# Graph layer with a normalised residual: adjacency kept in DRAM as fp32r and loaded tile by tile, self projection kept in SBUF

## The chip, the cores and the metric

The kernel runs on one core of one Trainium2 chip. The metric is the device time of one execution in microseconds (us); the median of three runs of the kernel before is 1660.79 us (1660.56 to 1660.93).

## The reference

`x` is (8, 2048, 512), the adjacency `a` is 2048 x 2048 of 0 and 1 (the same for all batches), `W` is 512 x 1024. Everything is fp32.

```python
Wi, Wj = (W[:, :Din], W[:, Din:])
mi = jnp.einsum('bkd,od->bko', x, Wi)
mj = jnp.einsum('bkd,od->bko', x, Wj)
deg = a.sum(axis=1)
out = deg[None, :, None] * (mi + b) + jnp.einsum('ij,bjo->bio', a, mj)
x = _layernorm(x + out, axis=-1)
```

## The kernel before

A batch has 16 row tiles of 128 rows. For each of the 8 batches two stages follow one another on TensorE.

**Projection**, 16 tiles of two halves (h = 0 gives `mj`, h = 1 gives `mi`). To keep fp32 accuracy with fp32r products, `x` and `W` are split in high and low parts. A half has 4 cross products (L295) and 8 main products (L305, L307), all 128x128 by 128x512. ScalarE makes `x_hi` and `x_lo` (L380, L382), copies the cross products out of PSUM (L395) and rounds `mj` to `mj_hi` (L399); POOL makes `x_df` and `mj_lo` (L247, L252); VectorE splits x and combines `mj` and `mi` (L489, L492, L502, L510). `mi` is a single tile: SP stores it to a DRAM buffer (L193), and `combine_mi` waits for the store of the tile before (L509).

**Aggregation**, 16 tiles. Tile i multiplies 16 weight tiles of the transposed adjacency (`adjT[s]`, two buffers of 128 x 2048 fp32r, 1 MB) with `mj_hi` and `mj_lo`: 32 matmuls (L329) in one of two PSUM banks. The adjacency lies in SBUF as int8 (`adjT8`), and ScalarE widens one tile at a time (`widen`, L411) when the tile two before has been multiplied. SP loads `mi` back into `mi_in` (L177) and x into `r` (L180); POOL adds the bias to `mi_in` (L258); VectorE makes the residual (L538), then in `normalise` adds the PSUM result (L544), takes the statistics, waits for the root from ScalarE (`root`, L415) and scales; SP stores the tile (L225). TensorE's tile m waits for the sum of tile m-2 (L321).

In **batch 0** the adjacency also comes in: 64 chunks of 128 x 512 int32 (256 KB) through four buffers `adj_in` (L164). ScalarE casts each to int8 (`cast_chunk`, L406), VectorE adds it up for the degrees (`count_chunk`, L521, L524). Two chunks go with each projection tile, and the other 32 with the aggregation tiles by this list:

```python
AGG_CHUNKS = [0, 3, 3, 3, 3, 2, 2, 4, 4, 4, 4, 0, 0, 0, 0, 0]
```

Every engine's order is the order in the program text, for SP too: one list of waits and transfers. `load_chunk(c)` waits until ScalarE and VectorE have used chunk c-4 (L162, L163). In an aggregation tile, ScalarE casts that tile's chunks, widens, and then does `root`; VectorE counts the tile's chunks, then does the next residual and `normalise`.

Of the kernel before, what the change touches and what calls it, by code (L numbers as in the profile page):

```python
# [5 lines left out]
def bass_adj_resnorm(nc, x, xt, adjt, wt, b, out):  # L6
# [32 lines left out]
    with ctx:  # L39
# [9 lines left out]
        mi_dram = nc.dram_tensor("mi_dram", [TILES, P, DO], fp32, kind="Internal").ap()  # L49

        adjT8 = sb("adjT8", [P, NT, N], i8)
# [13 lines left out]
        mi = sb("mi", [P, DO], fp32)  # L65
        mi_in = [sb(f"mi_in{s}", [P, DO], fp32) for s in range(2)]
# [20 lines left out]
        w_stage = [r[0], r[1], r[2], r[3], mi_in[0], mi_in[1], deg_part, mi]  # L87
# [20 lines left out]
        mi_stored = sem("mi_stored")  # L108
        mi_loaded = [sem(f"mi_loaded{s}") for s in range(2)]
# [6 lines left out]
        adjT_ready = sem("adjT_ready")  # L116
# [14 lines left out]
        AGG_CHUNKS = [0, 3, 3, 3, 3, 2, 2, 4, 4, 4, 4, 0, 0, 0, 0, 0]  # L131
# [26 lines left out]
        @block.sync  # L158
        def _(sp):
            def load_chunk(c):  # L160
                if c >= AB:
                    sp.wait_ge(adj_cast, c - AB + 1)  # L162
                    sp.wait_ge(deg_part_ready, c - AB + 1)  # L163
                sp.dma_start(adj_in[c % AB][:, :], adjt[c // NT, c % NT]).then_inc(adj_loaded[c % AB], 16)  # L164

            sp.dma_start(x_raw[0][:, :], xt[0]).then_inc(x_loaded[0], 16)
            for c in range(DK, 2 * DK):
                sp.dma_start(w_stage[c][:, :], wt[c]).then_inc(w_loaded[c], 16)
            sp.dma_start(x_raw[1][:, :], xt[1]).then_inc(x_loaded[1], 16)
            for c in range(DK):  # L170
                sp.dma_start(w_stage[c][:, :], wt[c]).then_inc(w_loaded[c], 16)
# [4 lines left out]
            def load_mi(m, u):  # L176
                sp.dma_start(mi_in[u % 2][:, :], mi_dram[m]).then_inc(mi_loaded[u % 2], 16)  # L177

            def load_r(m, u):
                sp.dma_start(r[u][:, :], x_tiles[m]).then_inc(r_loaded[u], 16)  # L180

            def batch(bt):
                zero = known(bt) and bt == 0
                base = NT * bt

                def proj(g):
                    for u in range(GT):
                        n = base + GT * g + u
                        if zero:
                            for c in range(PROJ_CHUNKS * (GT * g + u), PROJ_CHUNKS * (GT * g + u + 1)):  # L190
                                load_chunk(c + AB)
# [3 lines left out]
                over_groups(sp, zero, False, proj)  # L195

                sp.wait_ge(mi_stored, 16 * (base + 2))
                for u in range(2):
                    load_mi(base + u, u)
                for u in range(GT - 1):  # L200
                    if not zero:
                        sp.wait_ge(out_stored[u], 16 * NG * bt)
                    load_r(base + u, u)

                def agg(g):
                    for u in range(GT):
                        i = GT * g + u
                        m = base + i
                        begin = known(g) and g == 0
                        ending = known(g) and g == NG - 1  # L210
                        if begin and u == 0:
                            sp.wait_ge(mi_stored, 16 * (base + NT))
# [24 lines left out]
            for u in range(GT):  # L237
                sp.wait_ge(out_stored[u], 16 * NG * NB)

        @block.gpsimd  # L240
        def _(pool):
# [14 lines left out]
            def add_bias(m, u, turn):  # L256
                pool.wait_ge(mi_loaded[u % 2], turn)
                pool.tensor_tensor(mi_in[u % 2][:, :], mi_in[u % 2][:, :], bias[:, :], ALU.add).then_inc(mib_ready, 1)  # L258
# [3 lines left out]
            def batch(bt):  # L262
# [13 lines left out]
                with pool.Fori(0, NP) as k:  # L276
                    for u in range(2):
                        add_bias(NT * bt + 2 * k + u, u, 16 * (NP * bt + k + 1))
# [4 lines left out]
        def _(pe):  # L283
# [34 lines left out]
            def aggregate(bt, i, s, first, wait_free):  # L318
# [15 lines left out]
            def batch(bt):  # L334
# [13 lines left out]
                if zero:  # L348
                    for i in range(NT):
# [6 lines left out]
                        aggregate(0, i, i % 2, i == 0, i >= 2)  # L356
                else:
                    for i in range(2):
                        aggregate(bt, i, i, i == 0, True)
                    with pe.Fori(1, NP) as k:  # L360
                        for i in range(2):
                            aggregate(bt, 2 * k + i, i, False, True)
# [8 lines left out]
        def _(act):  # L371
# [52 lines left out]
            def batch(bt):  # L424
# [3 lines left out]
                def proj(g):  # L428
                    last_group = known(g) and g == NG - 1
                    for u in range(GT):  # L430
# [13 lines left out]
                        if last_group and u in (0, 2):  # L444
                            widen(u // 2, u // 2, NT if zero else None)

                over_groups(act, zero, True, proj)
                if zero:
                    for i in range(NT):
                        for c in agg_chunks(i):  # L450
                            cast_chunk(c)
                        if i < NT - 2:
                            act.wait_ge(agg_done, i + 1)
                            widen(i + 2, i % 2, NT * ((i + 2) // TPB + 1))
                        root(i)
                else:
                    with act.Fori(0, NP - 1) as k:
                        for i in range(2):
                            m = NT * bt + 2 * k + i
                            act.wait_ge(agg_done, m + 1)  # L460
                            widen(2 * k + i + 2, i, None)
                            root(m)
                    for i in range(2):
                        root(NT * bt + NT - 2 + i)
# [4 lines left out]
        def _(dve):  # L469
            def split_w(c, order):  # L470
# [5 lines left out]
                nc.vector.tensor_scalar(top[:, :].bitcast(u32), w_stage[c][:, :].bitcast(u32),  # L476
                                        HI_BITS, None, ALU.bitwise_and).then_inc(w_top_ready, 1)
                dve.wait_ge(w_top_ready, order + 1)
                nc.vector.tensor_tensor(W_lo[:, c, :], w_stage[c][:, :], top[:, :], ALU.subtract).then_inc(w_lo_ready, 1)  # L479
# [25 lines left out]
            def combine_mi(n):  # L505
                dve.wait_ge(main_done, 2 * n + 2)
                dve.wait_ge(cross_ready, 2 * n + 2)
                if not (known(n) and n == 0):
                    dve.wait_ge(mi_stored, 16 * n)  # L509
                nc.vector.scalar_tensor_tensor(mi[:, :], main_ps[1][:, :], 1.0 + 1.0 / S, cross[1][:, :],  # L510
# [22 lines left out]
            def residual(m, i, u, turn):  # L533
# [4 lines left out]
                nc.vector.scalar_tensor_tensor(r[u][:, :], mi_in[u % 2][:, :], deg[:, bass.ds(i, 1)], r[u][:, :],  # L538
# [35 lines left out]
            def batch(bt):  # L574
# [3 lines left out]
                def proj(g):  # L578
                    for u in range(GT):
# [7 lines left out]
                        combine_mi(n)  # L587
# [67 lines left out]
```

## Time and profile before

| What | us |
|---|---|
| median of the runs | 1660.79 |
| the profiled execution | 1659.85 |
| its span, first to last instruction | 1658.0 |
| TensorE busy | 1639.1 |
| VectorE busy | 851.4 |
| ScalarE busy | 665.0 |
| POOL busy | 504.9 |

The span is the time from the first to the last instruction of the profiled execution; its own time has 1.85 us around that. The granted TensorE clock is 0.996 of full speed in the mean. The DMA engines moved 187.26 MB, at 113 GB/s in the mean. A busy share says how much an engine worked, and not that the end waits for it: the chain that ended last and the waits tell that.

### The profile page before, as it was taken

The page shows a single profiled execution, that of the slowest core. Times are in us where ns is not written, and L with a number is a line of the kernel's source. Part 1 is how long each engine was busy: PE and PEld are TensorE (multiplying, and loading weights), DVE is VectorE, ACT ScalarE, POOL GpSimd, SP SyncE. Part 2 cuts the span into 40 slices and gives each one's busy share as a digit, 9 for nine tenths or more (in the row PEclk, how much of TensorE's full clock was granted, in tenths as well). Part 3 has the DMA queues.
Part 4 walks back from the last instruction along what each step waited for, and adds up shares of the span by engine and source line. Part 5 has one row for each costly group of instructions (what it writes and reads, how often), then busy time and mean ns, then how long its engine had stood idle before and what let it go on. Part 6 is the DMA issues. An engine that isn't in the chain of part 4 may idle for free.

```text
span 1658.0 us, 24935 instructions
## 1 busy us (share of the span) xinstructions
PE 1639.1 (99%) x7248; PEld 1354.8 (82%) x7248; DVE 851.4 (51%) x1884; ACT 665.0 (40%) x970; POOL 504.9 (30%) x390
## 2 busy tenths in 40 slices
PE   7999999999999999999999999999999999999998
PEld 5888888888888888888888888888888888888886
DVE  7768754455444544444544554444454445444544
ACT  5665435423344323442345332453225533255221
POOL 2542124311343113431134311443114421144210
PEclk8999999999999999999999999999999999999999
DMA  5656522333224332333322432224322343232432
GB/s 172 190 185 221 187 81 89 126 115 101 81 97 126 108 108 76 101 127 108 98 85 94 128 106 95 90 93 133 109 87 89 101 129 105 82 102 82 127 114 70
DMA packets 102698, 187.26 MB, mean 113 GB/s; under 512 B 11408, under 2 KB 11408, under 8 KB 102672
## 3 DMA queue, kind: packets, MB, share of 16 engines
q1 hardware_dynamic: 84528, 153.92, 29.0%
q10 hardware_dynamic: 18144, 33.04, 6.5%
q8 instruction: 11, 0.18, 0.0%
q14 instruction: 15, 0.12, 0.0%
HBM read 119.80 MB, written 67.11 MB: 113 GB/s over the span
## 4 chain that ended last, share of the span: by engine, by line
PE 96%; DVE 1%; DMA 1%; issue 1%; ACT 0%; SPq 0%; POOL 0%; DVEq 0%; ACTq 0%
PE agg_ps L329 56%; PE main_ps L305 13%; PE main_ps L307 13%; PE cross_ps L295 13%; DMA mi_dram<-mi 1%; DVE W_lo L479 0%; DVE deg_part L524 0%; PE deg_ps L314 0%; DMA mi_in<-in_wt 0%; ACT x_lo L382 0%; DVE mj L476 0%; DVE cross L476 0%; DVE mi L510 0%; DVE deg_part L521 0%; DVE x_raw L492 0%
## 5 line engine op out<-in xcount | busy, mean ns | idle before, releaser
L329 PE MATMUL agg_ps<-mj_lo,adjT 128*128 128x512 f32 x2048 | 797.9, 390 | 0.0
L329 PE MATMUL agg_ps<-mj_hi,adjT 128*128 128x512 f32 x2048 | 797.8, 390 | 0.0
L411 ACT ACTIVATE adjT<-adjT 128x2048 fp32r (+1 forms) x128 | 245.3, 1917 | 552.1 <-PE agg_ps L329 552.1
L329 PEld LDWEIGHTS agg_ps<-mj_hi,adjT 128*128 128x128 f32 x2048 | 384.4, 188 | 79.9
L329 PEld LDWEIGHTS agg_ps<-mj_lo,adjT 128*128 128x128 f32 x2048 | 384.8, 188 | 79.3
L305 PE MATMUL main_ps<-W_hi,x_hi 128*128 128x512 f32 x1024 | 400.0, 391 | 1.4 <-DVE mi L510 1.4
L307 PE MATMUL main_ps<-W_lo,x_lo 128*128 128x512 f32 x1024 | 399.7, 390 | 0.0
L258 POOL TENSOR_TENSOR mi_in<-mi_in,bias 128x512 f32<-128x512 f32 x128 | 166.0, 1300 | 651.3 <-DMA mi_in<-mi_dram 651.3
L295 PE MATMUL cross_ps<-W_df,x_df 128*128 128x512 f32 x1024 | 275.8, 392 | 9.6 <-POOL x_df L247 8.2
L252 POOL TENSOR_TENSOR mj_lo<-mj,mj_hi 128x512 f32 (+1 forms) x128 | 172.4, 1347 | 277.6 <-ACT mj_hi L399 277.6
L544 DVE TENSOR_TENSOR r<-agg_ps,r 128x512 f32<-128x512 f32 x128 | 88.4, 691 | 316.7 <-PE agg_ps L329 316.6
L395 ACT ACTIVATE cross<-cross_ps 128x512 f32<-128x512 f32 x256 | 150.6, 588 | 214.5 <-PE cross_ps L295 210.3
L295 PEld LDWEIGHTS cross_ps<-W_df,x_df 128*128 128x128 f32 x1024 | 192.0, 188 | 52.4 <-issue 8.3
L247 POOL TENSOR_TENSOR x_df<-x_top,x_lo 128x512 fp32r<-128x512 f32 x128 | 166.3, 1299 | 203.9 <-ACT x_lo L382 203.6
L305 PEld LDWEIGHTS main_ps<-W_hi,x_hi 128*128 128x128 f32 x1024 | 192.7, 188 | 42.5 <-DVE mi L510 2.3
L307 PEld LDWEIGHTS main_ps<-W_lo,x_lo 128*128 128x128 f32 x1024 | 193.0, 188 | 40.0
L502 DVE SCALAR_TENSOR_TENSOR mj<-main_ps,cross 128x512 f32<-128x512 f32 x128 | 88.3, 690 | 206.2 <-PE main_ps L307 199.2
L510 DVE SCALAR_TENSOR_TENSOR mi<-main_ps,cross 128x512 f32<-128x512 f32 x128 | 88.5, 691 | 129.4 <-PE main_ps L307 109.1
L538 DVE SCALAR_TENSOR_TENSOR r<-mi_in,deg,r 128x512 f32<-128x512 f32 x128 | 96.5, 756 | 53.8 <-DMA r<-in_x 43.1
L380 ACT ACTIVATE x_hi<-x_top 128x512 fp32r<-128x512 f32 x128 | 80.8, 631 | 65.5 <-PE main_ps L307 63.8
L546 DVE BATCH_NORM_STATS2 stats<-r 128x6 f32<-128x512 f32 x128 | 88.9, 695 | 11.6
L492 DVE TENSOR_TENSOR x_raw<-x_raw,x_top 128x512 f32<-128x512 f32 x128 | 88.7, 693 | 4.4
(43 smaller groups left out, 586.5 us busy)
## 6 DMA issues: line engine op xcount, KB each, us to landing
mi_dram<-mi SPq DMA_DIRECT2D x128, 256.0 KB, 2.0
mi_in<-mi_dram SPq DMA_DIRECT2D x128, 256.0 KB, 2.7
r<-in_x SPq DMA_DIRECT2D x128, 256.0 KB, 2.7
out<-r SPq DMA_DIRECT2D x128, 256.0 KB, 2.0
x_raw<-in_xt ACTq DMA_DIRECT2D x126, 256.0 KB, 2.7
adj_in<-in_adjt SPq DMA_DIRECT2D x64, 256.0 KB, 3.1
r<-in_wt SPq DMA_DIRECT2D x4, 256.0 KB, 5.3
x_raw<-in_xt SPq DMA_DIRECT2D x2, 256.0 KB, 3.8
```

Source lines behind the costliest of these rows:

```text
L247: pool.tensor_tensor(x_df[s][:, :], x_top[:, :], x_lo[s][:, :].bitcast(fp32), ALU.subtract).then_inc(x_df_ready, 1)
L252: pool.tensor_tensor(mj_lo[:, bass.ds(t, 1), :].rearrange("p t d -> p (t d)"), mj[:, :], mj_hi[:, bass.ds(t, 1), :].rearrange("p t d -> p ...
L258: pool.tensor_tensor(mi_in[u % 2][:, :], mi_in[u % 2][:, :], bias[:, :], ALU.add).then_inc(mib_ready, 1)
L295: last = nc.tensor.matmul(cross_ps[h][:, :], x_df[s][:, k * P:(k + 1) * P], W_df[:, half * DK + k, :], start=(k == 0), stop=(k == DK - 1))
L305: nc.tensor.matmul(main_ps[h][:, :], x_hi[s][:, k * P:(k + 1) * P], W_hi[:, half * DK + k, :], start=(k == 0), stop=False)
L307: last = nc.tensor.matmul(main_ps[h][:, :], x_lo[s][:, k * P:(k + 1) * P], W_lo[:, half * DK + k, :], start=False, stop=(k == DK - 1))
L329: last = nc.tensor.matmul(agg_ps[s][:, :], adjT[s][:, j, :], part[:, j, :], start=(j == 0 and part is mj_hi), stop=(j == NT - 1 and part i ...
L395: nc.scalar.activation(cross[h][:, :], cross_ps[h][:, :], ACT.Copy).then_inc(cross_ready, 1)
L411: nc.scalar.activation(adjT[s][:, :, :], adjT8[:, :, bass.ds(i * P, P)], ACT.Copy).then_inc(adjT_ready, 1)
L492: nc.vector.tensor_tensor(x_raw[s][:, :], x_raw[s][:, :], x_top[:, :], ALU.subtract).then_inc(x_rest_ready, 1)
L538: nc.vector.scalar_tensor_tensor(r[u][:, :], mi_in[u % 2][:, :], deg[:, bass.ds(i, 1)], r[u][:, :], ALU.mult, ALU.add).then_inc(res_ready, 1)
L546: nc.vector.bn_stats(stats[:, :], r[u][:, :]).then_inc(ln_step, 1)
```

## The change

- `mi_dram`, `mi_in` and `adjT8` go. `mi` becomes 16 tiles in SBUF (32 KB a partition); `combine_mi` writes tile t of it without a wait for a store, POOL adds the bias in place, the residual reads it there. Three of the staging buffers for W are now slices of `mi`.
- In batch 0 `cast_chunk` makes fp32r instead of int8, into one of two buffers `adj_wide`; ScalarE then waits for its own cast and itself issues the store of the chunk to `adj_dram`, in four pieces a partition of 128 values (512 B) each. The cast of chunk c waits for the store of chunk c-2.
- `widen` goes. SP loads `adjT[s]` from `adj_dram` in two halves of 512 KB (rows of 4 KB): the first when half of the tile two before has been multiplied (a new semaphore, `half_done`), the second when all of it has. TensorE waits for the halves one by one. The last two tiles of a batch load tiles 0 and 1 of the next. In batch 0 the first two tiles are loaded behind projection tile 10, and a load waits until the chunks that it reads are stored.
- The first three `r` tiles of a batch are loaded ahead of SP's wait in the aggregation rather than behind its projection loop, which is gone.
- The chunks of batch 0 go with the aggregation tiles by another list.

```diff
-        AGG_CHUNKS = [0, 3, 3, 3, 3, 2, 2, 4, 4, 4, 4, 0, 0, 0, 0, 0]
+        AGG_CHUNKS = [0, 3, 3, 3, 3, 4, 4, 4, 4, 4, 0, 0, 0, 0, 0, 0]
...
+            def load_adjT(i, s, q, zero):
+                if zero:
+                    for w in range(2):
+                        sp.wait_ge(adj_stored[w], 16 * (NT * (i // TPB) + NP * (q + 1)) // 2)
+                sp.dma_start(adjT[s][:, NP * q:NP * (q + 1), :].bitcast(fp32),
+                             adj_dram[i, :, NP * q:NP * (q + 1), :]).then_inc(adjT_loaded[s][q], 16)
...
-                        sp.wait_ge(mi_ready, n + 1)
-                        sp.dma_start(mi_dram[n], mi[:, :]).then_inc(mi_stored, 16)
...
+                if zero:
+                    for t in range(NT):
+                        for c in range(PROJ_CHUNKS * t, PROJ_CHUNKS * (t + 1)):
+                            load_chunk(c + AB)
+                        if t == 10:
+                            for i in range(2):
+                                for q in range(2):
+                                    load_adjT(i, i, q, True)
...
-                        if not (ending and u >= GT - 2):
-                            sp.wait_ge(res_ready, m + 1)
-                            load_mi(m + 2, u)
+                        wraps = ending and u >= GT - 2
+                        if not (last_batch and wraps):
+                            sp.wait_ge(half_done, m + 1)
+                            load_adjT(u - 2 if wraps and u >= 2 else i + 2, u % 2, 0, zero and not wraps)
+                            sp.wait_ge(agg_done, m + 1)
+                            load_adjT(u - 2 if wraps and u >= 2 else i + 2, u % 2, 1, zero and not wraps)
...
-                pe.wait_ge(adjT_ready, m + 1)
+                pe.wait_ge(adjT_loaded[s][0], turn)
                 if first:
                     pe.wait_ge(mj_lo_ready, NT * bt + NT - 1)
                 for j in range(NT):
+                    if j == NP:
+                        pe.wait_ge(adjT_loaded[s][1], turn)
...
+                    if j == NP - 1:
+                        last.then_inc(half_done, 1)
                 last.then_inc(agg_done, 1)
...
             def cast_chunk(c):
-                s = c % AB
+                s, w = c % AB, c % 2
+                q, j = c // NT, c % NT
                 act.wait_ge(adj_loaded[s], 16 * (c // AB + 1))
-                q, j = c // NT, c % NT
-                nc.scalar.activation(adjT8[:, j, q * DO:(q + 1) * DO], adj_in[s][:, :], ACT.Copy).then_inc(adj_cast, 1)
-
-            def widen(i, s, chunks):
-                if chunks is not None:
-                    act.wait_ge(adj_cast, chunks)
-                nc.scalar.activation(adjT[s][:, :, :], adjT8[:, :, bass.ds(i * P, P)], ACT.Copy).then_inc(adjT_ready, 1)
+                if c >= 2:
+                    act.wait_ge(adj_stored[w], 16 * (c // 2))
+                nc.scalar.activation(adj_wide[w][:, :], adj_in[s][:, :], ACT.Copy).then_inc(adj_cast, 1)
+                act.wait_ge(adj_cast, c + 1)
+                act.dma_start(adj_dram[TPB * q:TPB * (q + 1), :, j, :].rearrange("t p i -> p t i"),
+                              adj_wide[w][:, :].bitcast(fp32).rearrange("p (t i) -> p t i", t=TPB)
+                              ).then_inc(adj_stored[w], 16)
...
-            def combine_mi(n):
+            def combine_mi(n, t):
                 dve.wait_ge(main_done, 2 * n + 2)
                 dve.wait_ge(cross_ready, 2 * n + 2)
-                if not (known(n) and n == 0):
-                    dve.wait_ge(mi_stored, 16 * n)
```

## Rows read from the trace of the kernel before

**Rows 1.** The page: busy time and instructions, and the chain that ended last.
```profile
PE 1639.1 (99%) x7248; PEld 1354.8 (82%) x7248; DVE 851.4 (51%) x1884; ACT 665.0 (40%) x970; POOL 504.9 (30%) x390
...
PE 96%; DVE 1%; DMA 1%; issue 1%; ACT 0%; SPq 0%; POOL 0%; DVEq 0%; ACTq 0%
```
**Rows 2.** The chain in order of time: start us, us, what.
```profile
109.55 7.25 PE agg_ps L329 x32
...
228.46 0.91 PE cross_ps L295 x4
...
518.96 116.05 PE agg_ps L329 x512
...
722.37 116.05 PE agg_ps L329 x512
```
**Rows 3.** Timeline of TensorE, projection of batch 0: start us, us, instruction.
```profile
37.64 1.07 PE L295 MATMUL cross_ps<-W_df,x_df 128*128 128x512 f32 x4
...
41.66 1.07 PE L295 MATMUL cross_ps<-W_df,x_df 128*128 128x512 f32 x4
...
92.31 1.07 PE L295 MATMUL cross_ps<-W_df,x_df 128*128 128x512 f32 x4
...
95.03 1.07 PE L295 MATMUL cross_ps<-W_df,x_df 128*128 128x512 f32 x4
...
98.50 1.08 PE L295 MATMUL cross_ps<-W_df,x_df 128*128 128x512 f32 x4
```
**Rows 4.** The waits: total us, how many, longest.
```profile
ACT adjT L411 <- PE agg_ps L329: 552.1, 109, 8.1
...
DVE mi L510 <- DMA mi_dram<-mi: 18.1, 12, 3.3
```
**Rows 5.** The page's groups: busy us, mean ns | idle before, and its releaser.
```profile
L411 ACT ACTIVATE adjT<-adjT 128x2048 fp32r (+1 forms) x128 | 245.3, 1917 | 552.1 <-PE agg_ps L329 552.1
```
**Rows 6.** Windows: length, busy of PE, PEld, DVE, ACT, POOL; PEclk, DMA share, GB/s.
```profile
8.00:9.00 1.00, 0.00 (x0) 0.00 (x0) 0.97 (x3) 0.15 (x1) 0.00 (x0) 1.00 1.06 399
...
146.00:153.00 7.00, 7.00 (x33) 5.79 (x32) 6.16 (x15) 3.82 (x5) 1.29 (x1) 1.00 0.80 257
...
183.00:190.00 7.00, 7.00 (x33) 5.80 (x32) 6.05 (x15) 4.59 (x6) 1.59 (x1) 1.00 0.82 241
...
316.00:432.00 116.00, 116.00 (x514) 96.12 (x513) 57.11 (x153) 29.91 (x29) 21.06 (x17) 1.00 0.35 109
```
**Rows 7.** Timeline of VectorE in an aggregation tile of a middle batch.
```profile
424.46 0.69 DVE L544 TENSOR_TENSOR r<-agg_ps,r 128x512 f32<-128x512 f32 x1 [3.00 <-PE agg_ps L329]
...
427.88 0.55 DVE L563 TENSOR_SCALAR r<-r,mean_var,inv_std 128x512 f32<-128x512 f32 x1
```
**Rows 8.** DMA issues: count, KB each, median us from issue to landing.
```profile
r<-in_x SPq DMA_DIRECT2D x128, 256.0 KB, 2.7
out<-r SPq DMA_DIRECT2D x128, 256.0 KB, 2.0
...
adj_in<-in_adjt SPq DMA_DIRECT2D x64, 256.0 KB, 3.1
```
**Rows 9.** Timeline of ScalarE and its queue in a projection tile of batch 0.
```profile
52.80 0.63 ACT L380 ACTIVATE x_hi<-x_top 128x512 fp32r<-128x512 f32 x1 [0.24 <-PE main_ps L307]
53.34 0.62 ACT L382 ACTIVATE x_lo<-x_raw 128x512 fp32r<-128x512 f32 x1
...
53.98 0.33 ACTq L386 DMA_DIRECT2D x_raw<-in_xt  x1
...
56.37 0.60 ACT L395 ACTIVATE cross<-cross_ps 128x512 f32<-128x512 f32 x1 [1.37 <-PE cross_ps L295]
```
**Rows 10.** Timelines of ScalarE and VectorE, tiles with four chunks, batch 0.
```profile
171.56 0.20 ACT L415 ACTIVATE std<-var_eps 128x1 f32<-128x1 f32 x1
...
176.84 0.69 DVE L544 TENSOR_TENSOR r<-agg_ps,r 128x512 f32<-128x512 f32 x1
...
184.10 0.69 DVE L544 TENSOR_TENSOR r<-agg_ps,r 128x512 f32<-128x512 f32 x1
```

More of the change, by code:

```diff
@@ L64, in bass_adj_resnorm @@
         mj = sb("mj", [P, DO], fp32)
-        mi = sb("mi", [P, DO], fp32)
-        mi_in = [sb(f"mi_in{s}", [P, DO], fp32) for s in range(2)]
+        mi = sb("mi", [P, NT, DO], fp32)
+        adj_wide = [sb(f"adj_wide{s}", [P, DO], fp32r) for s in range(2)]
         r = [sb(f"r{s}", [P, D], fp32) for s in range(GT)]
@@ L85, in bass_adj_resnorm @@
         deg_ps = pb("deg_ps")
-        w_stage = [r[0], r[1], r[2], r[3], mi_in[0], mi_in[1], deg_part, mi]
+        w_stage = [r[s][:, :] for s in range(4)] + [mi[:, NT - 3, :], mi[:, NT - 2, :], deg_part[:, :], mi[:, NT - 1, :]]
         w_top = [mj, cross[1]]
@@ L107, in bass_adj_resnorm @@
         mi_ready = sem("mi_ready")
-        mi_stored = sem("mi_stored")
-        mi_loaded = [sem(f"mi_loaded{s}") for s in range(2)]
+        adj_stored = [sem(f"adj_stored{s}") for s in range(2)]
         r_loaded = [sem(f"r_loaded{s}") for s in range(GT)]
@@ L115, in bass_adj_resnorm @@
         deg_ready = sem("deg_ready")
-        adjT_ready = sem("adjT_ready")
+        adjT_loaded = [[sem(f"adjT_loaded{s}{q}") for q in range(2)] for s in range(2)]
+        half_done = sem("half_done")
         zeroed = sem("zeroed")
@@ L183, in batch @@
                 zero = known(bt) and bt == 0
+                last_batch = known(bt) and bt == NB - 1
                 base = NT * bt
[L186 to L191, printed above, removed]
-                        sp.wait_ge(mi_ready, n + 1)
-                        sp.dma_start(mi_dram[n], mi[:, :]).then_inc(mi_stored, 16)
[L195 to L199, printed above, removed]
+                if zero:
[6 more added lines that the diff above has]
+                                    load_adjT(i, i, q, True)
                 for u in range(GT - 1):
@@ L202, in batch @@
                         sp.wait_ge(out_stored[u], 16 * NG * bt)
+                    else:
+                        sp.wait_ge(w_ready, 2 * DK)
+                        sp.wait_ge(w_hi_ready, 2 * DK)
                     load_r(base + u, u)
@@ L254, in rest_of_mj, with add_bias @@
                                    ALU.subtract).then_inc(mj_lo_ready, 1)
-            def add_bias(m, u, turn):
-                pool.wait_ge(mi_loaded[u % 2], turn)
-                pool.tensor_tensor(mi_in[u % 2][:, :], mi_in[u % 2][:, :], bias[:, :], ALU.add).then_inc(mib_ready, 1)
+            def add_bias(m, i):
+                pool.wait_ge(mi_ready, m + 1)
+                own = mi[:, bass.ds(i, 1), :].rearrange("p t d -> p (t d)")
+                pool.tensor_tensor(own, own, bias[:, :], ALU.add).then_inc(mib_ready, 1)
             difference(0, 0)
@@ L277, in batch @@
                     for u in range(2):
-                        add_bias(NT * bt + 2 * k + u, u, 16 * (NP * bt + k + 1))
+                        add_bias(NT * bt + 2 * k + u, 2 * k + u)
             over_batches(pool, batch)
@@ L316, in degrees, with aggregate @@
                 last.then_inc(deg_in_psum, 1)
-            def aggregate(bt, i, s, first, wait_free):
+            def aggregate(bt, i, s, turn, first, wait_free):
                 m = NT * bt + i
@@ L355, in batch @@
                             degrees(3)
-                        aggregate(0, i, i % 2, i == 0, i >= 2)
+                        aggregate(0, i, i % 2, 16 * (i // 2 + 1), i == 0, i >= 2)
                 else:
                     for i in range(2):
-                        aggregate(bt, i, i, i == 0, True)
+                        aggregate(bt, i, i, 16 * (NP * bt + 1), i == 0, True)
                     with pe.Fori(1, NP) as k:
                         for i in range(2):
-                            aggregate(bt, 2 * k + i, i, False, True)
+                            aggregate(bt, 2 * k + i, i, 16 * (NP * bt + k + 1), False, True)
             pe.wait_ge(zeroed, 2)
@@ L451, in batch @@
                             cast_chunk(c)
-                        if i < NT - 2:
-                            act.wait_ge(agg_done, i + 1)
-                            widen(i + 2, i % 2, NT * ((i + 2) // TPB + 1))
                         root(i)
                 else:
[L457 to L464, printed above, removed]
+                    with act.Fori(0, NT) as i:
+                        root(NT * bt + i)
             over_batches(act, batch)
@@ L503, in combine_mj @@
                                                ALU.mult, ALU.subtract).then_inc(mj_ready, 1)
-            def combine_mi(n):
+            def combine_mi(n, t):
                 dve.wait_ge(main_done, 2 * n + 2)
                 dve.wait_ge(cross_ready, 2 * n + 2)
-                if not (known(n) and n == 0):
-                    dve.wait_ge(mi_stored, 16 * n)
-                nc.vector.scalar_tensor_tensor(mi[:, :], main_ps[1][:, :], 1.0 + 1.0 / S, cross[1][:, :],
+                nc.vector.scalar_tensor_tensor(mi[:, bass.ds(t, 1), :].rearrange("p t d -> p (t d)"), main_ps[1][:, :], 1.0 + 1.0 / S, cross[1][:, :],
                                                ALU.mult, ALU.subtract).then_inc(mi_ready, 1)
@@ L586, in proj @@
                             count_chunk(PROJ_CHUNKS * t)
-                        combine_mi(n)
+                        combine_mi(n, t)
                         if zero:
```

19 lines of the change are left out of this document (6 added, 13 removed).

## Prediction

> **What bounds the kernel now.** I read first the busy shares and the chain that ended last: TensorE is busy 1639.1 of 1658.0 us and holds 96% of the chain [rows 1]. So only what makes TensorE wait, or its work longer, counts. Next the chain in order of time, in a middle batch: from one aggregation's start to the next are 203.41 us, and its 512 matmuls take 116.05 [rows 2], that is 0.2267 us each and 7.25 us for a tile of 32. A projection tile has 24, 5.44 us. A batch of both is 16 x 12.69 = 203.1 us, so a middle batch has 0.3 us to give. All 7168 by 0.2267 are 1625 us; the 33 that are left lie at both ends of the kernel and in batch 0. The instructions, their shapes and the form of the weights in SBUF don't change, so I leave the 0.2267.
>
> Then TensorE's own timeline in batch 0. A half of a projection tile takes 2.72 us (95.03 - 92.31); twice it takes more, 41.66 - 37.64 = 4.02 and 98.50 - 95.03 = 3.47 [rows 3], together **2.05 us** lost. The waits say why: VectorE waited 18.1 us in 12 waits for the store of the single `mi` tile (L509) [rows 4], and the rest of that was covered. The longer waits beside it, ScalarE 552.1 us before the widening, are of an engine with time to spare.
>
> **The change, part by part.**
>
> *The widening (L411) goes.* 128 copies by 1.917 us are 245 us of ScalarE [rows 5]. TensorE never waits for them in a middle batch, where the period is the pure matmul time. Worth 0. The cover is TensorE itself.
>
> *The round trip of `mi` goes.* 128 stores and 128 loads of 256 KB leave SP's queue, and L509's wait goes: -2.05 us, all of it in batch 0. The store is late there because SP issues it behind adjacency chunks whose buffers it waits for. What is late next is the adjacency traffic below. The bias additions on POOL have the same number and now run back to back behind the projection; they stand beside VectorE work that in a middle batch waits for TensorE at each tile. 0 us.
>
> *The load of adjT, middle batches.* 256 issues of 512 KB replace the 256 of `mi`, so SP's issue time is no longer than before. Rate: 109 GB/s now in the aggregation [rows 6]; 16 loads of `mi` (4.2 MB in 116 us, 36 GB/s) go and 16.8 MB (145 GB/s) come: 218 GB/s, while 399 GB/s is shown for loads alone [rows 6]. Timing: SP does everything in order, so the first half of tile m+3 stands behind the store of tile m. That store is ready 3.97 us after the sum of m starts (427.88 + 0.55 - 424.46) [rows 7], so the load goes out at about +4.4 us and is needed at +14.5 (two tiles on). A 256 KB load lands in 2.7 us [rows 8]; half a tile adds another 0.7 us: 3.4 against 10 us. The second half has some 11 us. Tiles 0 and 1 of the next batch are fetched in the last two tiles of this one. 0 us.
>
> *Batch 0, projection.* ScalarE gets 32 stores. Each must wait until its own cast has ended (the starts of two ACTIVATEs are 0.54 apart and one takes 0.63, so 0.1 us) and issue; issuing took 0.33 us for the x load [rows 9]. Two chunks a tile add 0.9 us to an engine that idles 0.24 + 1.37 us a tile [rows 9]: covered, 0 us. Queued behind are the cross copies that TensorE's next half needs, so the bound from above is an issue four times as long (four times as many rows): 2.8 us a tile, 1.2 over, 19 us in 16 tiles. I take the 0.33, the one issue on this queue that a row shows. At the eleventh tile SP issues four half tiles ahead of the chunk loads: 2 MB, 5.6 us at the rate below, so a chunk lands after 3.1 + 5.6 = 8.7 us, and the four buffers give 4 x 2.72 = 10.9. 0 us, with 2.2 left.
>
> *Batch 0, aggregation.* Here I see the price. Count in pieces of 256 KB. A tile with four chunks has 4 chunk loads, 4 chunk stores, 4 for the next adjT tile, 1 for r and 1 for out; five tiles in a row have that. Before, with neither the stores nor the adjT loads beside them, the DMA share was already 0.80 and 0.82 at 257 and 241 GB/s [rows 6]. Four tiles have three chunks. Two prices are unknown. (a) The time of 256 KB with the DMA engines full: 0.66 us by the 399 GB/s of loads alone, 0.81 by the mixed row (257 / 0.80 = 321 GB/s). I take **0.70**, nearer the first, since reads outnumber stores. (b) What a store in rows of 512 B costs against one in rows of 2 KB; the trace has none. From below 1; from above 4, a short row as dear as a long one. The nearest row, the 2 KB-row store with 2.0 us to landing [rows 8], is mostly latency and not transfer, so I stay near the lower end: **1.25**. So with four chunks 10 + 5 = 15 pieces x 0.70 = 10.5 us against 7.26 of TensorE, 3.24 over, five times 16.2; with three chunks 9 + 3.75 = 12.75 x 0.70 = 8.93, 1.67 over, four times 6.7. Together the DMA engines fall **22.9 us** behind.
>
> The Trainium skill (DMA: Bandwidth & Descriptors, Why small descriptors are slow) gives about three bus cycles of overhead a packet at 32 bytes a cycle; an estimate by it is 76 / 67 = 1.13 for (b), the lag 20.2 and the end 1672. The same page (Specifications) puts HBM for one core at about 358 GB/s; the trace's 399 over one us disagrees, and with 358 the estimate would be 1679.
>
> How much lag is covered: the cast waits for the store two chunks back, `root(i)` is queued behind the casts on ScalarE, VectorE's normalise waits for root, the next sum is behind it, and TensorE's tile i+3 waits for that sum (L321). In batch 0 the root at 171.56 is followed by the sum at 176.84, done at 177.53; tile 10 needs it when tile 9 ends, at about 184.1 [rows 10]. **6.5 us** of cover. Nothing regains lag in between: at four chunks VectorE's own sums stand 7.25 us apart with no idle time noted before the two later ones [rows 10]. TensorE stalls 22.9 - 6.5 = 16.4 us, between tiles 6 and 12 of batch 0.
>
> **Sum.** -2.05 + 16.4 = +14.3 us. The profiled execution took 1659.85 us (1.85 around the span) and the median is 0.94 above it; 1659.85 + 14.3 = 1674.2, and on the median's footing **1675 us**, 0.9% slower.
>
> **Rivals.**
> *The cover holds (not slower).* For: at 0.66 us a piece and a factor of 1 the lag is (14 x 0.66 - 7.26) x 5 + (12 x 0.66 - 7.26) x 4 = 12.5 us, and part of it is adjT halves that can themselves be 7 us late without harm. It decides where the lag stays under about 8 us. Then -2.05 and up to 2 us of stall: 1659 to 1661 us. Against: it needs the best rate seen for 65 us on end. Chance 0.25. Within it lies the case that all is hidden, 1658.7; a gain over 0.2% would need 3.3 us, and rows give only the 2.05.
> *ScalarE's two store buffers set the pace, not the volume.* A chunk takes (cast 0.62 + 0.1 + issue 0.33 + landing) / 2. With the 2.0 of the 2 KB-row store it is 1.5 us, under the 1.8 that four chunks a tile allow; with 4 us (my estimate for the load there, from the 3.1 of a chunk load now [rows 8] and the traffic that comes) 2.5. Then 10.1 - 7.26 = 2.9 x 5 and 0.3 x 4, 15.5 - 6.5 = 9, less 2.05: 1668 us. Longest waits would be ScalarE's, for the stores, with the DMA share well below 1. Chance 0.20.
> *Short rows are dear.* Factor 2 and 0.81 a piece: (18 x 0.81 - 7.26) x 5 + (15 x 0.81 - 7.26) x 4 = 56 us, less 8.5: 1708 us. The DMA share would stay at 1 from tile 1 to 12. Chance 0.15.
>
> **How the numbers follow.** Forecast 0.40, rivals 0.25, 0.20, 0.15. About 0.2% (3.3 us) is what a measurement can tell. The first rival is nearly all "within", with 0.03 for a gain that I don't see; the others end slower, but 0.02 of the second may stay within: faster 0.03, same 0.24, slower 0.73. The range goes from the first rival's best case, 1658, to 1698, between the forecast and the dear store; what is left out is 0.12 above and a little below.
>
> **What would show it.** Right: middle batches still at 203.4 us a period; batch 0's aggregation at 130 to 140 us instead of 118.9 (228.46 - 109.55 [rows 2]), with TensorE's idle time before L321's tiles 6 to 12, DMA share near 1 there, ScalarE's casts waiting for chunk stores; projection of batch 0 some 2 us shorter. Wrong: a longer middle period (then a half tile is late and SP's order is to blame), stalls already in the projection (ScalarE's issue is dear, or the four early half tiles), or TensorE without gaps in batch 0, which would mean that the engines carry 500 GB/s or that the lag allowed is far more than 6.5 us.

## The result, and the profile after

The changed kernel takes **1700.7 us** (median of four runs, 1697.99 to 1702.47) against 1660.67 us before, measured beside it: a ratio of 1.0241, 95% interval 1.0225 to 1.0256. It is slower by 40 us. The forecast was slower, by 14 us, with a range that ended at 1698.

The page of the kernel after: the busy times, the chain that ended last, and the issues with their landing times.

```profile
span 1697.3 us, 24739 instructions
...
PE 1651.1 (97%) x7248; PEld 1360.9 (80%) x7248; DVE 906.7 (53%) x1884; ACT 426.3 (25%) x842; POOL 509.3 (30%) x390
...
PE 87%; DMA 6%; DVE 2%; issue 1%; ACT 1%; POOL 1%; DVEq 0%; ACTq 0%; POOLq 0%; SPq 0%
...
adjT<-adj_dram SPq DMA_DIRECT2D x256, 512.0 KB, 4.2
r<-in_x SPq DMA_DIRECT2D x128, 256.0 KB, 4.2
out<-r SPq DMA_DIRECT2D x128, 256.0 KB, 2.2
...
adj_dram<-adj_wide ACTq DMA_DIRECT2D x64, 256.0 KB, 4.3
```

Beside [rows 1] the 39.3 us of span split in two without a remainder. TensorE is busy 12.0 us longer for the same 7248 instructions (1651.1 - 1639.1), and idle 27.3 us longer (46.2 against 18.9). The ScalarE time of the widening is gone as computed (426.3 against 665.0), and bought nothing. DMA work, 1% of the chain before, is 6% of it.

Where in time? The chain of the kernel after in order of time (start us, us, what): the first batch's end and three aggregations of middle batches.

```profile
266.81 0.91 PE cross_ps L299 x4
...
353.91 116.07 PE agg_ps L335 x512
557.50 116.07 PE agg_ps L335 x512
761.06 116.07 PE agg_ps L335 x512
```

Batch 1 starts at 266.81 instead of 228.46 [rows 2]: **38.4 us are lost in batch 0**. A middle batch has a period of 203.56 us (761.06 - 557.50) instead of 203.41, some 0.15 us more seven times, 1 us. So doubling the traffic of the middle batches' aggregation cost next to nothing, as forecast. Within batch 0, the first matmul of the aggregation starts at 110.5 us instead of 109.4: 1.1 us are lost in the projection and some 37 in the aggregation, which takes 156.3 us (266.81 - 110.5) instead of 118.9.

In batch 0 the longest waits, from the table of waits of the kernel after (total us, times, longest):

```profile
ACT adj_wide L416 <- DMA adj_dram<-adj_wide: 76.2, 34, 7.4
...
DVE inv L549 <- ACT std L424: 66.0, 128, 7.1
...
PE agg_ps L335 <- DMA adjT<-adj_dram: 21.4, 7, 5.5
```

ScalarE waits 76 us for its own chunk stores, VectorE for the root that is queued behind them (66 us, where 34 us is its ordinary sum of 0.27 us a tile), and TensorE, last, for adjT. One turn of that wheel, from the timeline of all engines in a tile with four chunks:

```profile
178.16 1.54 SPq L179 DMA_DIRECT2D adjT<-adj_dram  x2
...
181.89 0.63 ACT L416 ACTIVATE adj_wide<-adj_in 128x512 fp32r<-128x512 int32 x1 [1.87 <-DMA adj_dram<-adj_wide]
...
187.86 0.63 ACT L416 ACTIVATE adj_wide<-adj_in 128x512 fp32r<-128x512 int32 x1 [5.34 <-DMA adj_dram<-adj_wide]
...
189.28 0.20 ACT L424 ACTIVATE std<-var_eps 128x1 f32<-128x1 f32 x1 [0.78 <-ACT adj_wide L416]
...
190.35 0.55 DVE L559 TENSOR_SCALAR r<-r,mean_var,inv_std 128x512 f32<-128x512 f32 x1
...
190.93 0.34 SPq L228 DMA_DIRECT2D out<-r  x1
191.38 1.39 SPq L179 DMA_DIRECT2D adjT<-adj_dram  x2
```

Read it downwards. The cast at 187.86 waited 5.34 us for the store two chunks back. The root at 189.28 stands behind it; the scaling, the store of the output and, since SP takes everything in order, **the load of the next adjT tile** stand behind the root. That load leaves at 191.38, 13.2 us after the one before, and what follows on TensorE is this (its own timeline; the number in brackets is the idle time before):

```profile
191.45 0.39 PE L335 MATMUL agg_ps<-mj_lo,adjT 128*128 128x512 f32 x1
197.37 0.76 PE L335 MATMUL agg_ps<-mj_hi,adjT 128*128 128x512 f32 x1 [5.54 <-DMA adjT<-adj_dram]
197.93 0.63 PE L335 MATMUL agg_ps<-mj_lo,adjT 128*128 128x512 f32 x1
198.36 0.63 PE L335 MATMUL agg_ps<-mj_hi,adjT 128*128 128x512 f32 x1
```

TensorE idles 5.54 us, and the next matmuls start 0.43 us apart instead of 0.23: the granted clock is at its lower level (1.2 of 2.4 GHz) behind the pause. This is where the 12 us of longer busy time are from: the trace's record of the clock has it at the lower level for 23.9 us in all between 162 and 241 us, where the kernel before has none, and half of that is 12.0 us. Not every pause did it: behind one of 2.76 us, at 184.33, the matmuls were 0.23 us apart.

The first stall is earlier than tile 6, where the forecast had it: tile 3 of batch 0 starts at 135.39 after 2.06 us of waiting for VectorE's sum, and tile 4 at 144.45 after 1.51 us of waiting for adjT.

Two windows of batch 0's aggregation in the kernel after, 30 us of it and most of it (length, busy of PE, PEld, DVE, ACT, POOL, then PEclk, DMA share, GB/s):

```profile
140.00:170.00 30.00, 24.73 (x95) 19.61 (x95) 19.05 (x45) 5.55 (x12) 0.00 (x0) 0.89 1.04 344
113.00:230.00 117.00, 95.00 (x386) 76.06 (x385) 65.27 (x136) 22.79 (x43) 22.87 (x16) 0.91 0.90 281
```

The DMA engines are shown as 90% busy over the 117 us, yet move 281 GB/s, far from the 399 of [rows 6]. From the shares alone one could call the kernel bound by the volume, as the prediction did. The experiments say something else.

### The profile page after: what moved, and what is told of

Its sections match the earlier page's. It is cut to its first block, busy times and chain, and to the rows that moved or that the text cites. A ratio compares the mean times of both kernels' runs of the same rounds, so it can differ in the third digit from the quotient of the medians.

```text
span 1697.3 us, 24739 instructions
## 1 busy us (share of the span) xinstructions
PE 1651.1 (97%) x7248; PEld 1360.9 (80%) x7248; DVE 906.7 (53%) x1884; ACT 426.3 (25%) x842; POOL 509.3 (30%) x390
## 3 DMA queue, kind: packets, MB, share of 16 engines
q10 hardware_dynamic: 51936, 49.82, 10.1%
## 4 chain that ended last, share of the span: by engine, by line
PE 87%; DMA 6%; DVE 2%; issue 1%; ACT 1%; POOL 1%; DVEq 0%; ACTq 0%; POOLq 0%; SPq 0%
PE agg_ps L335 50%; PE cross_ps L299 13%; PE main_ps L309 12%; PE main_ps L311 12%; DMA adj_dram<-adj_wide 6%; ACT adj_wide L416 1%; POOL x_df L250 1%; DVE W_lo L477 0%; ACT x_lo L390 0%; DVE stats L542 0%; DVEq L541 0%; DMA adjT<-adj_dram 0%; DVE r L540 0%; ACTq L418 0%; DMA mi<-in_wt 0%
## 5 line engine op out<-in xcount | busy, mean ns | idle before, releaser
L335 PE MATMUL agg_ps<-mj_hi,adjT 128*128 128x512 f32 x2048 | 804.1, 393 | 23.4 <-DMA adjT<-adj_dram 21.4
L335 PEld LDWEIGHTS agg_ps<-mj_lo,adjT 128*128 128x128 f32 x2048 | 388.2, 190 | 80.9
L424 ACT ACTIVATE std<-var_eps 128x1 f32<-128x1 f32 x128 | 26.0, 203 | 874.7 <-DVE var_eps L546 871.5
L262 POOL TENSOR_TENSOR mi<-mi,bias 128x512 f32 x128 | 175.1, 1405 | 0.0
L506 DVE SCALAR_TENSOR_TENSOR mi<-main_ps,cross 128x512 f32 (+1 forms) x128 | 88.4, 691 | 123.4 <-PE main_ps L311 118.2
L534 DVE SCALAR_TENSOR_TENSOR r<-mi,deg,r 128x512 f32<-128x512 f32 x128 | 125.1, 982 | 19.7 <-POOL mi L262 15.5
```

The costliest lines, as they stand in the source:

```text
L262: pool.tensor_tensor(own, own, bias[:, :], ALU.add).then_inc(mib_ready, 1)
L534: nc.vector.scalar_tensor_tensor(r[u][:, :], mi[:, bass.ds(i, 1), :].rearrange("p t d -> p (t d)"), deg[:, bass.ds(i, 1)], r[u][:, :], ALU ...
```

## The experiments

Three theories of the 38 us: the volume (V), the pacing of ScalarE by two store buffers (P), and the short rows of the stores (S). Beside them a burst of bias additions on POOL (B), seen in the trace after, and the bunch of early tile loads. The kernel after itself ranged over 4.5 us in its four runs (1697.99 to 1702.47), so where a run stands alone, differences of less than about 5 us from it show nothing.

**Four store buffers.**

```diff
-        adj_wide = [sb(f"adj_wide{s}", [P, DO], fp32r) for s in range(2)]
+        adj_wide = [sb(f"adj_wide{s}", [P, DO], fp32r) for s in range(WB)]
...
-                if c >= 2:
-                    act.wait_ge(adj_stored[w], 16 * (c // 2))
+                if c >= WB:
+                    act.wait_ge(adj_stored[w], 16 * (c // WB))
```

(with `WB = 4`, a semaphore for each buffer, and SP's waits on them to match)

> Four adj_wide buffers instead of two, so a cast waits for the store four chunks back. The changed kernel has 40 us more than before, all in batch 0 (its aggregation, first product to the next batch's first, takes about 154 us instead of 119), and in it ScalarE waits 76 us for stores. Theory V (volume: the DMA engines are full and a piece of 256 KB costs about 0.9 us in this mix, so about 13 us per tile with four chunks): the waits move elsewhere, the time stays within 1698 to 1702 us, the period of the four-chunk tiles stays 12.5 to 13.5 us. Theory P (pacing: two store buffers with 4 to 8 us of landing): the period falls towards 10 us, total 1675 to 1685 us, and ScalarE's waits for the stores fall below 20 us.

Measured: 1674.35 us in one run, the kernel before beside it 1658.95. The same kernel in several runs:

> The kernel with four adj_wide buffers again, timed in rounds, since single looks differ by some us. It gave 1674.35 once; 1673 to 1678 us and a ratio of 1.008 to 1.011 to the kernel before are expected by all theories.

Measured: 1675.07 us (1673.83 to 1676.89), ratio 1.0089, interval 1.0072 to 1.0106. Against 1700.7, some **26 us of the 40** are gone with the bytes, the transfers and their order unchanged. The waits and two windows of the first of these runs:

```profile
ACT adj_wide L417 <- DMA adj_dram<-adj_wide: 4.0, 3, 2.2
...
PE agg_ps L336 <- DMA adjT<-adj_dram: 2.8, 4, 1.2
```

```profile
140.00:170.00 30.00, 28.94 (x129) 23.15 (x129) 19.28 (x48) 6.81 (x14) 0.00 (x0) 1.00 1.06 382
113.00:230.00 117.00, 106.39 (x464) 85.50 (x463) 79.60 (x172) 22.53 (x46) 20.78 (x15) 0.99 0.95 326
```

ScalarE's wait for stores falls from 76.2 to 4.0 us and TensorE's for adjT from 21.4 to 2.8. The same DMA engines now carry 382 GB/s over the 30 us (344 before the edit) and 326 over the 117 us (281): with two buffers they didn't give what they can, whatever their share says, 1.04 against 1.06 and 0.90 against 0.95. Their packets took longer instead. The DMA queues from 113 to 205 us (packets, MB, share of 16 engines; q1 is SP's, q10 ScalarE's, which has only chunk stores there), first of the kernel after, then with four buffers (the second of these runs):

```profile
q1 hardware_dynamic: 8673, 19.99, 66.0%
...
q1 hardware_dynamic: 10064, 23.56, 69.7%
q10 hardware_dynamic: 15103, 7.50, 27.6%
```

By these rows 256 KB on SP's queue cost 0.80 us of all 16 engines with two buffers (66.0% of 92 us for 19.99 MB) and 0.71 with four. A single store did not land sooner (median 5.3 us with four buffers, 4.3 with two); there are just more of them under way. TensorE's clock stays at 0.99 in the window (0.91 before the edit), and its busy time is 1643.4 instead of 1651.1 us. P holds, with a total just under or at its lower end of 1675 us; V as the cause of the whole falls.

**Long rows in the store.**

```diff
-                act.dma_start(adj_dram[TPB * q:TPB * (q + 1), :, j, :].rearrange("t p i -> p t i"),
+                act.dma_start(adj_dram[TPB * q + j % TPB, :, TPB * (j // TPB):TPB * (j // TPB) + TPB, :],
```

> Each chunk is stored as one contiguous row of 2 KB per partition instead of four rows of 512 B; the bytes, the number of transfers and all waits stay. The values land at other places of adj_dram, so the aggregation multiplies permuted adjacency tiles. Theory S (short rows make the stores dear): stores land in 2 to 3 us instead of 4.3, total 1675 to 1685 us. Theory V with a factor near 1.1 for short rows: 4 pieces of 15 get 10% cheaper, 0.4 us a tile, total 1695 to 1700 us. Theory P expects what the landing time gives: no change if it stays above 4 us.

Measured: 1691.91 us in one run, some 9 us under the kernel after and between what S and V gave. The stores didn't land sooner in the median (4.5 us), but the longest took 8.9 us instead of 11.1, the mean of the last sixteen was 5.1 us instead of 5.7, and ScalarE's waits for stores fell from 76.2 to 63.5 us. So once more with four buffers, in one run and then in several beside the short rows:

> Four adj_wide buffers and each chunk stored as one row of 2 KB per partition (the values land at other places, so the adjacency tiles are permuted). With two buffers the long rows gave some 8 us, with short ones four buffers gave 26 us. If short rows cost DMA time by themselves (a factor of 1.1 to 1.25 on 4 of 15 pieces, 0.3 to 0.7 us a tile), 1668 to 1672 us; if they acted only through the landing time that two buffers wait for, no change from 1674.

> Four buffers and chunk stores in 2 KB rows, timed in rounds beside the former. It gave 1677.81 once. If short rows cost DMA time by themselves, it must come out 2 to 6 us under the former; if they acted only through the landing time that two buffers wait for, the two are equal within 2 us.

Measured: 1677.81 us, and in several runs 1677.55 (1676.73 to 1678.39), ratio 1.0103 (1.0086 to 1.0120), against 1675.07 and 1.0089 for the short rows. The long rows gain nothing in the total. Both expectations took it that DMA time, if the short rows cost any, would show there. The trace says that they do cost it. The queues from 113 to 205 us, with long rows:

```profile
q1 hardware_dynamic: 9923, 22.93, 70.3%
q10 hardware_dynamic: 4079, 7.41, 22.1%
```

256 KB of chunk stores take 0.72 us of all 16 engines in rows of 2 KB and, by the rows above, 0.89 in rows of 512 B: **a factor of 1.23, which doesn't show in the total**. The DMA share in that window falls from 0.98 to 0.93 with the long rows, the rate from 338 to 331 GB/s, and TensorE is no busier (80.9 against 81.5 us); why nothing is gained stays open. With two buffers the long rows act through the landing times that ScalarE waits for.

**Thin tile loads in batch 0.**

```diff
-                sp.dma_start(adjT[s][:, NP * q:NP * (q + 1), :].bitcast(fp32),
-                             adj_dram[i, :, NP * q:NP * (q + 1), :]).then_inc(adjT_loaded[s][q], 16)
+                n = 1 if zero and not whole else NP
+                sp.dma_start(adjT[s][:, NP * q:NP * q + n, :].bitcast(fp32),
+                             adj_dram[i, :, NP * q:NP * q + n, :]).then_inc(adjT_loaded[s][q], 16)
```

(`whole` is set for the four early half tiles)

> In the aggregation of batch 0 each adjT half load moves only its first weight tile of 128x128 (64 KB instead of 512 KB); the rest of the buffer stays what it was, so batch 0 is multiplied with stale weights. Order, waits and the stores stay. It takes 4 pieces of about 14 out of each tile by 3.5. Theory V: with 10.5 to 11 pieces the DMA share falls below 1 and the period to about 9 us at most: total 1665 to 1672 us. Theory P: the stores land faster without the tile loads beside them, but with two buffers the four-chunk tiles stay above 9 us: total above 1675 us. The VectorE delay by POOL's burst of bias additions (first two tiles, 13 us between two sums) stays in both.

Measured: 1674.46 us in one run, 26 us less as well. So both levers work alone: with 12.9 MB taken away the stores land in a median of 3.9 us and ScalarE's wait falls to 45.9 us. It lies between what V gave (up to 1672) and P (above 1675); P took the landing time as less bound to the traffic than it is.

The kernels with two buffers let P be checked in numbers. It says that a cast comes every (1.05 + landing) / 2 us, 1.05 being cast, wait and issue. For the last sixteen casts of batch 0 (177.09 to 227.52 us in the kernel after) the mean landing times, the steps by the formula and the measured steps are: kernel after 5.71, 3.38, 3.36 us; long rows 5.08, 3.07, 3.09; thin loads 3.86, 2.45, 2.42. Of the kernels further down the one with POOL paced has 5.78, 3.41, 3.45, the one with the early loads spread 5.44, 3.24, 3.28, and the one with the old list 4.96, 3.01, 3.28; in that one ScalarE also waited 8.3 us for chunk loads.

Four buffers and thin loads together:

> Four adj_wide buffers and the adjT half loads of batch 0's aggregation cut to 64 KB (stale weights in batch 0). If pacing by two buffers and the volume of the tile loads are all that costs, the two together leave only the delay by POOL's burst and the projection: 1659 to 1664 us. If the two don't add (one wait hides behind the other), it stays near the 1674 that each alone gave.

Measured: 1665.50 us in one run. The two don't add (26 + 26 would be 52, more than is lost) but whichever comes second still takes 9 us. The row of the window:

```profile
113.00:230.00 117.00, 114.17 (x507) 94.05 (x506) 84.79 (x187) 22.74 (x47) 21.43 (x15) 0.99 0.73 231
```

TensorE is busy 114.2 of 117 us, 95.0 in the kernel after. So the volume does matter once the pacing is gone: about 9 to 10 us (1674.35 or 1675.07 against 1665.50, where 1674.35 and 1665.50 are one run each). With the volume taken out first it is the pacing that has 9 us left (1674.46 against 1665.50). So the 26 us can't be given to one of them: they are what two buffers and the landing times under that traffic cost together.

**The list of chunks of the kernel before**, `[0,3,3,3,3,2,2,4,4,4,4,...]`:

> The chunk list of the kernel before (0,3,3,3,3,2,2,4,4,4,4) in the changed kernel: the same chunks, spread over ten tiles rather than nine. Theory V: the volume up to tile 12 is the same, so at most the cover is used better: total 1692 to 1700 us. A rival that the list itself (five four-chunk tiles in a row) is the cause: total below 1685 us.

Measured: 1697.03 us in one run, within the spread of the kernel after; ScalarE still waits 65.4 us for stores. The list is not the cause.

**POOL's bias additions, one tile at a time.**

```diff
-                with pool.Fori(0, NP) as k:
+                for u in range(2):
+                    add_bias(NT * bt + u, u)
+                with pool.Fori(1, NP) as k:
                     for u in range(2):
+                        pool.wait_ge(res_ready, NT * bt + 2 * k + u)
                         add_bias(NT * bt + 2 * k + u, 2 * k + u)
```

> The changed kernel, in which POOL adds the bias to tile m only when the residual of tile m-1 is done, instead of 16 additions back to back behind the projection. In the changed kernel VectorE needs 13 us from the first sum to the second in batch 0, beside that burst. Theory B (the burst uses up the cover of 6.5 us before the chunk stores come): the first two sums stand 7 to 8 us apart, TensorE starts to stall later, total 1692 to 1697 us. Rival (the stores set the pace anyway and TensorE catches up with them): within 2 us of 1700.

Measured: 1698.01 us in one run. The first half of theory B is right. The first two sums of batch 0, in the timeline of VectorE, of after:

```profile
121.72 0.68 DVE L540 TENSOR_TENSOR r<-agg_ps,r 128x512 f32<-128x512 f32 x1
...
134.66 0.68 DVE L540 TENSOR_TENSOR r<-agg_ps,r 128x512 f32<-128x512 f32 x1
```

and with the edit:

```profile
119.76 0.68 DVE L543 TENSOR_TENSOR r<-agg_ps,r 128x512 f32<-128x512 f32 x1
126.69 0.69 DVE L543 TENSOR_TENSOR r<-agg_ps,r 128x512 f32<-128x512 f32 x1 [0.75 <-PE agg_ps L338]
```

12.9 us become 6.9. VectorE's total busy time falls by 63 us (906.7 to 843.3) when the additions no longer run side by side with it. But the total doesn't move beyond the spread of the kernel after: ScalarE waits 89.5 us for stores instead of 76.2, so the time gained in the first tiles is waited out behind them. The rival was right about the total.

**The early half tiles, one per projection tile.**

```diff
-                        if t == 10:
-                            for i in range(2):
-                                for q in range(2):
-                                    load_adjT(i, i, q, True)
+                        if 10 <= t < 14:
+                            load_adjT((t - 10) // 2, (t - 10) // 2, (t - 10) % 2, True)
```

> The changed kernel with its two store buffers, but the four early half tiles issued one each at projection tiles 10 to 13. In the changed kernel one cast waits 6.45 us for a store that went out beside the 2 MB issued at tile 10, and the aggregation of batch 0 starts some 5 us later than its matmuls need. If the bunch is the cause, that wait falls below 2 us and the total to 1694 to 1697 us; if the stall only moves into the aggregation, it stays within 2 us of 1700.

Measured: 1692.77 us in one run, some 8 us less and 5 under the fastest run of the kernel after; the expectation had 1694 to 1697. The aggregation of batch 0 starts at 107.4 us instead of 110.5 (109.6 to 112.0 in the other kernels with two buffers), so 3 us of it are shown to come from the projection; the rest is not traced. The wait of 6.45 us beside the bunch, which the trace of after has in the projection, is 0.88 us at that chunk; others of 1.0 and 2.4 us come up behind it, so the expectation of less than 2 us held for that chunk only. ScalarE's waits in total are nearly what they were (74.3 us).

**Four buffers, POOL paced and the early loads spread, together.**

> Four adj_wide buffers, POOL's bias additions paced by the residuals, and the four early half tiles issued one per projection tile (10 to 13) instead of all at tile 10. With four buffers alone it was 1674.35. If the burst of POOL and the bunch of early loads each cost what the traces show (up to 6.5 us of cover, and some us of chunk loads behind 2 MB), 1664 to 1670 us; if the volume alone is left to decide, 1672 to 1675 us. Not under 1661 by any theory.

Measured: 1669.46 us (1667.22 to 1671.10), ratio 1.0053, interval 1.0038 to 1.0069. It is the best form of the change that was tried, and still slower than the kernel before. TensorE's waits left in it are 4.1 us for adjT and 2.8 us for a sum; ScalarE waits 33.6 us for chunk loads instead of chunk stores (6.4 us). With the burst of POOL and the bunch of early loads gone, 5.6 us less than with four buffers alone, where pacing POOL by itself had moved nothing clear: it counts once the stores don't set the pace.

More than four buffers are not measured: eight don't fit in SBUF beside the rest (a tile of 2048 B a partition finds 1888 B left). Expected were 1672 to 1676 us if four had used up the pacing, and 4 us less if not.

**The expected gain alone**, in the kernel before:

```diff
-        mi = sb("mi", [P, DO], fp32)
+        mi = [sb(f"mi{s}", [P, DO], fp32) for s in range(2)]
...
-                    dve.wait_ge(mi_stored, 16 * n)
+                    dve.wait_ge(mi_stored[u % 2], turn)
```

(`turn` is the number of stores of that buffer so far, times 16)

> The kernel before with two mi tiles and a store semaphore for each, so combine_mi waits for the store two tiles back; the adjacency stays int8 in SBUF. This is the one gain that the prediction gave the change, alone: 2.05 us of TensorE idle in the projection of batch 0. If that is right, 1.5 to 2.5 us under the kernel before, a ratio of 0.9985 to 0.9991. Rival (the store is late for SP's queue and stays late with two tiles): no difference.

Measured: 1657.46 us (1657.29 to 1658.73), ratio **0.9982**, interval 0.9973 to 0.9991. It beats both kernels. TensorE's wait for `mi` in the kernel before, and all the waits of TensorE in this one (the first two stand before its first products):

```profile
PE main_ps L305 <- DVE mi L510: 1.4, 2, 1.0
...
PE cross_ps L297 <- POOL x_df L249: 8.3, 1, 8.3
PE cross_ps L297 <- DVE W_df L483: 1.8, 1, 1.8
PE agg_ps L369 <- POOL ones L245: 1.1, 1, 1.1
```

The gain is 3.1 us in the median, and the interval (1.5 to 4.5 us) takes in the 2.05 that the rows gave.

## Why the prediction was right or wrong

- **Bound by TensorE, and the middle batches have nothing to give or to lose: right.** 203.56 us a period for 203.41. The 0.15 us has no cause found: it is also there with POOL paced (759.70 - 556.14 = 203.56 in that run's chain).
- **The widening is worth 0: right.** ScalarE has 239 us less work, and TensorE's idle time in middle batches is unchanged.
- **The wait for the single `mi` tile, -2.05 us: right**, as the kernel with two `mi` tiles shows. It is in the changed kernel too: with the early loads spread, the aggregation of batch 0 starts 2.0 us sooner than in the kernel before (107.4 against 109.4). In the kernel after the bunch of early loads takes it back (110.5).
- **Batch 0's projection at no cost: wrong.** The issue costs what was taken (0.38 us, not four times 0.33). But the reckoning of the early half tiles looked at the chunk loads behind them on SP's queue, and not at ScalarE's chunk stores, which share the DMA engines with them: one waited cast stood 6.45 us in front of the cross copies. Spreading the loads moved the start of the aggregation by 3.1 us.
- **Price (a), 0.70 us for 256 KB: right.** 382 GB/s over 30 us with four buffers are 0.69 us. **Price (b), 1.25 for short rows: right as DMA time,** 1.23 by the queues' rows with four buffers, though nothing of it shows in the total there. The estimate of 1.13 by the Trainium skill (DMA: Bandwidth & Descriptors, Why small descriptors are slow) is too low for these stores. The 358 GB/s for one core that the same page has (Specifications) is exceeded here, by the 382 over 30 us.
- **"The DMA engines fall 22.9 us behind": the step that failed.** This sum has prices that held and assumes engines that are always fed. They weren't: with two buffers and a landing time that grows with the traffic, ScalarE could not keep enough stores under way. From 177.09 to 227.52 us the kernel after made 16 casts in 15 steps of 3.36 us, behind a mean landing time of 5.7 us, where the second rival put 4 and the forecast let the casts' wait for stores set no pace. Four steps are 13.4 us a tile against the 10.5 of the volume sum, and the aggregation of batch 0 took 156 us where 130 to 140 were forecast. The rival that had the mechanism had 0.20, and was priced at 1668 because its landing time was too short: with 5.7 us its own sum gives 13.5 - 7.26 = 6.2 five times and 10.1 - 7.26 = 2.9 four times, 42.7 less 6.5 and 2.05, about 1695 us (an estimate from these rows). It was wrong in expecting a DMA share well below 1. The forecast's volume is real; with four buffers it is worth about 9 us. That the kernel with four buffers takes 1675.07 us, the number that was forecast, is luck in part: it also holds the burst of POOL and the bunch of early loads, and without them it is 1669.46.
- **The cover of 6.5 us: worked out on a way that did not decide.** TensorE waited 21.4 us for adjT and 2.1 us for a sum, so the cover was not put to the test. (By the timeline it is 6.3 rather than 6.5: tile 10 starts at 183.8 in the kernel before, and 184.1 is where VectorE's sum behind tile 9 starts.) The late root holds up SP's output store, and behind that store the next tile's load: the prediction had noted this order for middle batches, and not followed it in batch 0. In addition POOL's burst used 6 us of cover in the first two tiles, so that tile 3 already waited; the prediction had priced it at 0 by looking at middle batches alone. By itself that changes little (1698.01).
- **The clock: left out.** Of the 39.3 us of span, 12.0 are TensorE's work at the lower clock behind pauses of up to 5.5 us. The price of such a stall is the pause and the slow matmuls behind it, together.

## What to carry to other kernels

When a change adds a store with its own buffers on an engine's queue, price it twice: the bytes at the full rate, and the steps at (compute + issue + landing under load) / buffers; take the larger. The landing time has to be that under the load to come: here an output store of 256 KB had landed in 2.0 us, and chunk stores of the same size took 5.7 in the mean under the new traffic. Where no row has it, work the sum out for several landing times and see where it starts to bite. A DMA share near 1 does not say that the bytes are at their limit; compare the GB/s with the best stretch that any run shows. And before a round trip through DRAM is replaced to get rid of a wait, try one more buffer in front of the wait: here it gave the whole gain (3.1 us), and none of the traffic.

## What the runs showed that had not been expected

- The same traffic ran at 281 GB/s with a DMA share of 0.90 and at 326 with 0.95, by the number of store buffers alone; over 30 us at 344 with 1.04 and at 382 with 1.06.
- With two store buffers the mean landing time gives the step of the casts to 0.04 us in five of six kernels, from 3.86 us of landing and 2.42 a step to 5.78 and 3.45.
- Stores of 256 KB to DRAM took 1.23 times the DMA time in rows of 512 B as in rows of 2 KB (0.89 and 0.72 us of all 16 engines), and still the kernel with them was no slower (1675.07 against 1677.55 us, both with four buffers). With two buffers the long rows took some 9 us off, in one run.
- 16 bias additions of POOL back to back made VectorE's work beside them longer: 63 us of busy time over the kernel (906.7 against 843.3 with the additions paced), and 12.9 us instead of 6.9 between two sums.
- A pause of 5.54 us of TensorE was followed by matmuls 0.43 us apart instead of 0.23. Altogether the lower clock was 12.0 of 39.3 us.
